# A longer warm-up of all 128 rows, the second item's chain ahead, and the bulk loads behind the first stacks

## What is computed

```python
x = x + attn_a(layernorm(x))   # 16 heads, rotary positions, softmax
x = x + ffn(layernorm(x))      # silu(x Wg) * (x Wu) Wd, integer weights / 127
x = x + attn_b(layernorm(x))   # 16 heads, causal, sparsemax
x = x + ffn(layernorm(x))
# attn: q, k, v = x W + b; scores = q k^T * scale; probs v; output projection
# q = q * cos + rotate_half(q) * sin, and so k (attn_a only)
```

## Time and profile before

| | us |
|---|---|
| median of 3 runs | 600.16 |
| lowest, highest | 597.83, 601.16 |
| profiled execution, device time | 598.14 |
| its span, first to last instruction | 596.4 |
| TensorE busy in it | 568.1 |

### The profile page before, as it was taken

One profiled execution on the slowest core, in us unless ns is written; L12 is line 12 of the kernel. 1 busy time (PEld: TensorE's weight loads), 2 busy tenths in 40 slices (PEclk: granted clock), 3 DMA queues, 4 the chain that ended last, 5 costly groups with the idle time before them and its releaser, 6 DMA issues.

```text
span 596.4 us, 19146 instructions
## 1 busy us (share of the span) xinstructions
PE 568.1 (95%) x6702; PEld 438.2 (73%) x6702; DVE 495.8 (83%) x1445; ACT 415.0 (70%) x1038; POOL 385.3 (65%) x817
## 2 busy tenths in 40 slices
PE   8778999999999999999999998999999999999895
PEld 6555666777777777777677786788888888888774
DVE  3679889898988898987788888788888899889763
ACT  1104678778887777788888767767887777777652
POOL 4755556667776667677667776666666677764422
PEclk9989999999999999999999999999999999999999
DMA  7656666566766666745545644335544445441000
GB/s 220 178 157 146 164 155 152 131 151 156 175 152 154 150 150 150 176 117 140 134 117 126 156 128 103 90 90 128 118 119 120 130 128 129 115 121 36 12 20 23
DMA packets 74657, 76.25 MB, mean 128 GB/s; under 512 B 10348, under 2 KB 68908, under 8 KB 70092
## 3 DMA queue, kind: packets, MB, share of 16 engines
q1 hardware_dynamic: 63636, 68.09, 45.0%
q10 hardware_dynamic: 10920, 6.88, 5.5%
HBM read 46.86 MB, written 23.33 MB: 118 GB/s over the span
## 4 chain that ended last, share of the span: by engine, by line
PE 70%; DVE 19%; issue 4%; ACT 3%; POOL 3%; DMA 1%; SPq 0%; ACTq 0%; DVEq 0%; POOLq 0%
PE banks L1630 15%; PE banks L1571 10%; PE banks L1606 9%; PE banks L1472 7%; PE banks L1535 7%; DVE top L1156 5%; DVE top L1155 3%; PE banks L1524 3%; DVE neg_shift L1150 2%; PE banks L1525 2%; PE banks L1504 2%; PE banks L1574 2%; DVE top_sums L1177 1%; DVE top_sums L1180 1%; PE banks L1482 1%
## 5 line engine op out<-in xcount | busy, mean ns | idle before, releaser
L1366 ACT ACTIVATE probs_t<-banks 128x512 f32<-128x512 f32 (+1 forms) x496 | 259.2, 551 | 72.3 <-PE banks L1606 47.8
L1150 DVE TENSOR_REDUCE neg_shift<-banks 128x2 f32<-128x512 f32 x256 | 165.7, 681 | 31.5 <-PE banks L1571 30.0
L1630 PE MATMUL banks<-probs_t,v_ext 128*32 128x256 f32 (+1 forms) x2048 | 116.8, 357 | 0.0
L1571 PE MATMUL banks<-k_stack,q_stack 72*128 72x256 bf16 x512 | 99.7, 276 | 8.0 <-DVE neg_shift L1150 3.3
L1156 DVE MAX8 top<-banks 128x8 f32<-128x256 f32 x256 | 106.1, 414 | 0.0
L1606 PE MATMUL banks<-q_stack,k_stack 75*128 75x256 bf16 x512 | 98.4, 273 | 0.3 <-ACT probs_t L1366 0.2
L1155 DVE MAX8 top<-banks 128x8 f32<-128x128 f32 x256 | 74.1, 290 | 19.8 <-PE banks L1580 19.4
L1026 POOL TENSOR_TENSOR hidden<-up_tanh,gate_half 128x256 f32<-128x256 f32 x93 | 68.3, 736 | 28.6 <-DVE up_tanh L1209 23.5
L1630 PEld LDWEIGHTS banks<-probs_t,v_ext 128*32 128x32 f32 x2048 | 55.4, 109 | 38.8 <-issue 12.8
L1571 PEld LDWEIGHTS banks<-k_stack,q_stack 72*128 72x128 bf16 x512 | 40.4, 98 | 48.1 <-DVE neg_shift L1150 36.4
L1524 PE MATMUL banks<-f_xT_high,w_gate_up 128*128 128x256 f32 x192 | 57.5, 322 | 2.3 <-DVE up_tanh L1209 2.0
(11 more groups left out here) (123 smaller groups left out, 1366.9 us busy)
## 6 DMA issues: line engine op xcount, KB each, us to landing
q_stack<-q_image SPq DMA_DIRECT2D x93, 192.0 KB
k_stack<-k_image SPq DMA_DIRECT2D x93, 192.0 KB
q_image<-qk_parts SPq DMA_DIRECT2D x32, 192.0 KB, 2.4
k_image<-qk_parts SPq DMA_DIRECT2D x32, 192.0 KB, 2.1
q_image<-qk_parts SPq DMA_DIRECT2D x32, 128.0 KB, 2.9
o_image<-out_t SPq DMA_DIRECT2D x32, 128.0 KB, 1.8
out_compact<-o_image SPq DMA_DIRECT2D x32, 64.0 KB
rdenominators<-r_image SPq DMA_DIRECT2D x16, 128.0 KB, 3.5
```

The costliest lines, as they stand in the source:

```text
L1150: dve.tensor_reduce(m.nm[:, n % STACKS, h, :], scores.rearrange("p (q k) -> p q k", q=TT), AX.X, ALU.max, negate=True).then_inc(reduced, 1)
L1366: act.activation(m.pt[:, (n * Q + g) % GROUPS, i, 0:size], shifted_bank(n, j)[:, 0:size], ACT.Exp if is_soft(n) else ACT.Relu, scale=SCALE ...
L1571: ins = pe.matmul(scores[:, qt * T:(qt + 1) * T], qs[0:STACK, h, qt * P:(qt + 1) * P], ks[0:STACK, h, :], start=True, stop=True)
L1630: ins = pe.matmul(out_bank[32 * i:32 * i + 32, at + skip:at + T], v_windows(v, kt)[:, Q * g + i, :], m.pt[:, (n * Q + g) % GROUPS, i, kt * ...
```

## The change

```diff
-ONCE = dict(set_v=-14, ones=-31, bulk=-22, sum_bias=20, fold_bias=22, cast_masks=24, cast_weights=40)
+ONCE = dict(set_v=-17, ones=-31, bulk=-22, masks=-11, weights=14, sum_bias=20, fold_bias=22, cast_masks=24, cast_weights=40)
-WARM_UP = 24
-SPARE = {-16: 46, -10: 10}
+WARM_UP = 28
+SPARE = {-23: 4, -17: 4, -13: 78}
-SECOND = dict(a_bn=-17, a_aggr=-17, a_rstd=-17, a_norm=-16, xT=-15, q=-14, cos_q=-14, sin_q=-14,
-              k=-13, cos_k=-13, sin_k=-13, v=-10, take_v=-9, split_q=-13, split_k=-12, store_q=-7, load_q=-5,
-              store_k=-5, load_k=-2)
+SECOND = dict(a_bn=-27, a_aggr=-27, a_rstd=-26, a_norm=-23, xT=-17, q=-15, cos_q=-15, sin_q=-15,
+              k=-14, cos_k=-14, sin_k=-14, v=-13, take_v=-12, split_q=-14, split_k=-13, store_q=-7, store_k=-6,
+              load_q=-5, load_k=-4)
+    warm_rows = m.pt[:, 0, 0, 0:T // 2].bitcast(BF16)
+            sp.dma_start(m.x[:, TT:NEAR * TT, :], x_d[:, TT:NEAR * TT, :]).then_inc(x_near_loaded, SEM)
             sp.dma_start(m.cc[:, CC["cos"]:CC["invk"]], io["consts"][:, CC["cos"]:CC["invk"]]).then_inc(rope_loaded, SEM)
             sp.dma_start(m.wa[:, WA["v"]:], io["wa"][:, WA["v"]:]).then_inc(wvo_loaded, SEM)
-            sp.dma_start(m.x[:, TT:NEAR * TT, :], x_d[:, TT:NEAR * TT, :]).then_inc(x_near_loaded, SEM)
+            pool.memset(warm_rows, 1.0).then_inc(warm_set, 1)
             pool.memset(m.neghalf[:, :], -0.5).then_inc(consts, 1)
             def load_weights():
                 act.dma_start(m.wb[:, :], io["wb"]).then_inc(wb_loaded, SEM)
+
+            def load_masks():
+
+                act.wait_ge(first_k_loaded, PARTS * SEM)
                 act.dma_start(m.cc[:, CC["invk"]:], io["consts"][:, CC["invk"]:CC_COLS]).then_inc(masks_loaded, SEM)
                 act.dma_start(m.co[:, :], io["consts"][:, CC_COLS:]).then_inc(masks_loaded, SEM)
-                act.dma_start(m.wf_int[:, :], io["wf"]).then_inc(wf_loaded, SEM)
+                if step == ONCE["masks"]:
+                    load_masks()
+                if step == ONCE["weights"]:
+                    act.dma_start(m.wf_int[:, :], io["wf"]).then_inc(wf_loaded, SEM)
-            pe.wait_ge(ones_set, 1)
+            pe.wait_ge(warm_set, 1)
             for i in range(WARM_UP):
-                pe.matmul(shifted_banks[:, 1, 0:T], m.one_rows[:, 0:P], m.one_rows[:, :], start=True, stop=True)
+                pe.matmul(shifted_banks[:, 1, 0:T], warm_rows[:, 0:P], warm_rows, start=True, stop=True)
```

More of the change, by code:

```diff
@@ L683, in main_phase @@
     ones_set = sem("ones_set")
+    warm_set = sem("warm_set")
     mask_rows_cast = sem("mask_rows_cast")
```

## The result

| | before | after |
|---|---|---|
| median of 4 runs each, us | 599.0 | 605.93 |
| lowest, highest | 595.49, 601.16 | 602.05, 607.96 |
| profiled execution | 598.14 | 607.96 |
| its span | 596.4 | 606.2 |

The ratio is 1.0118, with a 95% interval of 1.0077 to 1.0158. The forecast was no change (600.0, range 597.0 to 602.4); the time lies above the range.

A forecast was written before the change was run, and what follows sets the result against it. TensorE, busy 568.1 of 596.4 us, bounds the kernel; only the start can change. Item 0 gains 1.5 us, but late loads keep item 1 at 37.5 instead of 37.55: sum 0.0, median 600.0 us, range 597.0 to 602.4.

The forecast's parts named there:

- The steady part is full: TensorE from 100 to 300 us: busy 199.47 of 200 us, so changes in the first 60 us arrive whole at the end.
- Part 1, the clock: Warm-up: 28 products of 128 rows raise the clock after 3.7 us and end at 6.05; rope step 1.7 us earlier.
- The rival that the 128 rows do nothing: Warm-up: clock still rises at about 10 us, warm-up ends at 7.3; total 600.6 to 602.3 us, chance 0.08.
- The first stack lands at 21.1: Item 0's gate: query store issued at 12.6, stack landed at 21.1, scores from 21.3, a gain of 1.5 us.
- Part 2: Second item's early chain: rows at 5.9 us, spares ending at 21.1 to 21.5, splits near 23, 4 us earlier but unusable.
- Part 3, the failed step: Masks and weights loaded behind the first stack: 1.6 and 1.4 us of engine time; item 1 starts at 37.5 us.
- Upper bound: Late bulk loads before item 1: all 3.0 us added to the 14.7 between the gates, item 1 at 38.8.
- The hole at 28 to 29 us: DMA share 0.07 while the queue awaited a store; added traffic fills it and its sides, 1.3 us less cost.
- Half clock again at the same cost: After the idling before item 1: 0.24 us a head, some 0.8 us, as in the kernel before.
- Rival 2: Second stack pushed out: masks and weights add fully, item 1 at 38.8, half clock longer; 602.1 us, chance 0.14.
- Rival 1: Bulk loads do not hurt: item 1 at 35.85; 598.3 us, down to 596.7 if the clock holds; chance 0.26.

The follow-up runs named there:

- e2: Changed kernel with masks and constants issued early again and without the wait, integer weights still late at step 14; median 597.55 us, ratio 0.9986.
- e17: Changed kernel with 10 spare products in place of 78; one run, item 0 at 20.61 us, item 1 at 39.87.
- e6: Changed kernel with masks early and the integer weights issued together with the second query load; median 600.38 us, ratio 1.0032.
- e7: Changed kernel with masks early, weights behind the second stack, 39 spares of 512 columns in place of 78 of 256; 600.92 us, ratio 1.0039.
- e12: e2 with GpSimd's fills of the value tiles later, at step -12 for -17; median 601.8 us, ratio 1.0047.
- e14: e2 with 10 spare products in place of 78; one run, item 0 at 22.14 us, item 1 at 36.33.
- e3: Changed kernel with masks and weights both early again, without the wait, keeping warm-up and early chain of item 1; 598.0 us, ratio 1.0002.
- e10: Kernel before with only the warm-up changed to 28 products of 128 rows; median 599.56 us, ratio 1.0024.
- e8: Kernel before with only masks and constants moved behind the first key stack and integer weights to step 14; 603.16 us, ratio 1.0071.
- e16: Kernel before with only the x pieces of items 8 to 15 moved to steps 60 and 76 from 27 and 43; 596.69 us, ratio 0.9971.
- e1: Changed kernel with the integer weights issued early again, masks still behind the first stack; median 600.98 us, ratio 1.0064.
- e5: Changed kernel with the integer weights issued only behind the second item's key stack, masks still late; median 600.44 us, ratio 1.0019.
- e11: Changed kernel, masks late, with the integer weights issued together with the second query load; median 602.42 us, ratio 1.0113.
- e18: e13 with the x rows of items 5 to 7 issued at step 31 in place of step 1; 595.04 us, ratio 0.9948.
- e13: e2 with the x pieces of items 8 to 15 at steps 60 and 76 in place of 27 and 43; 595.51 us, ratio 0.9954.

## Why item 0 gained nothing

**Ten spares instead of 78** on the changed kernel, and the same on e2.

```diff
-SPARE = {-23: 4, -17: 4, -13: 78}
+SPARE = {-23: 4, -17: 4, -13: 10}
```

> The changed kernel with 10 spare products in place of 78, and nothing else in flight at 13 to 16 us (in the other kernel with few spares a 384 KB x piece was issued at 13.9). Seven profiles with a fetch at 14.4 to 14.9 have the second part of item 0's query store landing 1.2 us after the fetch's end. If the fetch holds it: no fetch at 14 to 16 us, the first query load issued at 15.1 to 15.6, item 0 at 20.8 to 21.4. If not: load at 16.4 or later.

> Masks early, weights at step 14, 10 spare products behind the second item's values in place of 78. If the instruction fetch at 15 us, called by TensorE's progress through its program, holds back the first stores, it is not in the stretch of 14 to 16 us, the first query load is issued at 15.2 to 15.6 and item 0 starts at 20.8 to 21.5 (at half clock, TensorE having idled). Otherwise load at 16.3 to 17.2 and item 0 at 22.3 or later.

In after, the first query store is issued at 12.74, 1.5 us earlier than before, but the load behind it at 17.07, as late as before. The queues of after from 14 to 17 us:

```profile
q1 hardware_dynamic: 889, 0.43, 51.9%
q8 instruction: 1, 0.02, 1.9%
...
k_image<-qk_parts SPq DMA_DIRECT2D x1, 192.0 KB, 3.3
```

and of e17:

```profile
q1 hardware_dynamic: 1086, 0.63, 71.8%
...
k_image<-qk_parts SPq DMA_DIRECT2D x1, 192.0 KB, 2.0
```

One instruction fetch of 16 KB, at 14.92 us in after, holds one of sixteen engines for 1.9% of 16 x 3 us, 0.9 us. Of the thirteen profiles with a fetch between 14.4 and 15.8 us, eleven have the query store's second part landing 1.1 to 1.2 us after the fetch's end, whatever the time of the fetch; in the other two (e2, e6) it had landed before. I read that as the store's share on that engine waiting for the fetch. In e17 the fetch comes at 26.57. The query store's second part lands in 2.1 us instead of 3.9, the key store in 2.0 instead of 3.3. The query load goes out at 15.55 and item 0 starts at 20.61, 2.0 us earlier:

```profile
15.55 1.14 SPq L843 DMA_DIRECT2D q_stack<-q_image  x3
...
20.61 0.58 PE L1582 MATMUL banks<-k_stack,q_stack 72*128 72x256 bf16 x2 [6.43 <-DMA k_stack<-k_image]
```

Its window from there on:

```profile
20.60:26.50 5.90, 5.89 (x28) 4.09 (x29) 4.11 (x10) 0.00 (x0) 2.47 (x6) 0.50 0.96 272
```

But TensorE has idled 6.43 us, and the clock is at half for the first 5.9 us of the scores (last row). Wide spares (e7) and later fills (e12) left the fetch where it was, at 15 us, so it follows neither the fills nor the count of spares as long as their time is the same. It moved when 68 spares were left out and TensorE was through them some 7 us sooner; what ties the fetch to that is not shown. In e14 no fetch stood there either, but a piece of x was sent at 13.90, 0.9 us behind the store's second part, which took 3.4 us to land: load at 16.39, item 0 at 22.14. And in e3 the masks and weights, sent early, are still under way when the now earlier store goes out: its load is issued at 18.11, and item 0 starts at 24.61.

## Why the prediction was wrong, step by step

- *The steady part is full, and what is lost before 60 us arrives at the end*: right. +8.7 at item 1, +9.1 at item 4, +9.8 at the end.
- *Part 1, the clock*: right. 28 products in 5.36 us, ending at 6.46 (forecast 6.05), rope at 8.49 (8.1), query store at 12.74 (12.6). The rival that the 128 rows do nothing is refuted by e10 too, where nothing else was changed: 28 products in 4.7 us against 5.30 for 24 of 48 rows. It is no accident of one execution: in all seventeen profiles with 128 rows the 28 products took 4.55 to 5.93 us, less than the 6.2 of 28 products at half clock, and in all three with 48 rows (before, e8, e16) the 24 took 5.30, each at half clock. The rule of the Trainium skill behind the rival ("TensorE: Matmul & The Clock Gate", What's actually happening), which speaks of how busy TensorE is and not of rows, does not account for that.
- *"The first stack lands at 21.1", item 0 1.5 us earlier*: mis-sized, measured 0.2. I let the time from store to landed stack stay as it was; the fetch, which fell behind the store before, now falls on it. e17, without the fetch there, starts item 0 2.2 us earlier than the kernel before does.
- *Part 2*: right where it could be seen. Item 1's rows at 6.21 (5.9), spares ending at 21.34 (21.1 to 21.5), the last split ending at 23.0 (near 23). That the splits are not what the queue waits for is right too.
- *Part 3, the failed step*: "Upper bound: all 3.0 us are added" was no upper bound. Item 1 came at 46.24, 42.50 and 42.57 against 38.8. The sum took bulk traffic as engine time in one pile. The runs show a chain: the masks delay a store (4.7 us to land in e1, 5.8 in after, 2.1 in e2), so the load behind it is issued 2.3 us later (e1 against e2), which puts it behind the weights, and then its packets run slowly (these two together 4 to 7.5 us, after's profiles against e5). The hole at 28 to 29 us that I counted as 1.3 us of free room ended when exactly that store had landed, at 29.03. The masks did fill it, but in front of the store, and moved its landing, and the load behind it, from 29.05 to 30.27.
- *Half clock again at the same cost*: right in the changed kernel (15.1 us from item 1 to item 2, before 15.6).
- *Rival 2, the second stack pushed out*: the right mechanism, with 0.14 and a price of 2.1 us, where 6.9 (medians) to 9.8 (profiles) were measured. *Rival 1*, bulk that doesn't hurt, is what the weights alone do (e2). The spread between 20.2 and 23.6 us within the changed kernel was in none of the rivals.

What stays open is why the second stack's packets go on at 0.6 to 0.8 of their rate after the weights have landed. That goes with the weights being issued ahead of the load and not with both loads being late (e8, e11, e17), but no run changes that order alone, with the masks early, and e11's median is no better than the changed kernel's. So part 3 is shown as the cause, the delayed store as its first step, and the slow packets only as what was seen.

## What to carry to other kernels

A load that is put behind another stage's data must be checked against every store whose landing releases a load: in front of such a store, bulk costs its whole time in series, and the cost of two loads doesn't add up from their engine time. Before moving 1 MB, look for a window in which no gate's transfer is under way, as the share of 0.12 in e18 shows, and keep it a few microseconds away from the next issue, since a lead gained elsewhere lets the two meet. Most stalls of 2 us and more were followed here by several microseconds at half clock, so the price is more than the idling.

## What the runs showed of the hardware

- The clock rises under products of 128 rows and did not under 5.3 us of products of 48 rows. The 28 products of after took 5.36 us; at 221 ns each at half clock and 113 at full that is 20 and 8 of them, so the rise is at about 5.6 us. In e10 they took 4.68: 14 and 14, the rise at 4.2. After 6.4 us of idling it was at half for 5.9 us of work (e17), and 2.2 us of idling brought half clock as well, still there from 56 to 60 us (e2); idle times of 0.4 to 0.9 us, as in e13 and e18, did not. The length of one idle time does not decide it: 1.6 us in e10 (before 16.1) was followed by half clock from 17.8 to 21.1, 2.0 us in e3 (before 24.6) by full clock up to 28.
- A fetch of 16 KB of instructions takes one DMA engine for 0.9 us; with it stores in flight took 3.9 and 3.3 us to land, without it 2.1 and 2.0 (after, e17).
- DMA engines can be 86% busy at 111 GB/s; in the same stretch, with other traffic before it, 80% gave 182. The share alone doesn't tell what is moved.
- With identical code up to there, item 1 came at 46.24, 42.50 and 42.57. One profile of a transfer-bound stage is a sample.
